# Expert layers of a four-layer graph and mixture-of-experts kernel: wide first-layer products, summed on VectorE, two tiles ahead

## The reference

```
probs = softmax(xf @ gate_w + gate_b); top2_vals, top2_idx = top_k(probs, 2)
h = gelu(xf @ w1 + bb1)                # per expert: 256 -> H
y = h @ w2 + bb2                       # H -> 256
acc = acc + we[:, None] * y            # weight of this expert, 0 where it was not chosen
```

## Time and profile before

| | |
|---|---|
| median of three runs | 2801.65 us (2794.58 to 2802.57) |
| profiled execution: its own time, its span | 2792.34 us, 2790.5 us |
| TensorE busy | 2187.1 us, 78% |
| VectorE busy | 1557.0 us, 56% |
| ScalarE busy | 1131.6 us, 41% |
| GpSimd busy | 445.6 us, 16% |
| mean granted TensorE clock | 0.89 |

### The profile page before, as it was taken

One profiled execution on the slowest core, in us unless ns is written; L12 is line 12 of the kernel. 1 busy time (PEld: TensorE's weight loads), 2 busy tenths in 40 slices (PEclk: granted clock), 3 DMA queues, 4 the chain that ended last, 5 costly groups with the idle time before them and its releaser, 6 DMA issues. The chain is left out here.

```text
span 2790.5 us, 46760 instructions
## 1 busy us (share of the span) xinstructions
PE 2187.1 (78%) x16458; PEld 1556.5 (56%) x16458; DVE 1557.0 (56%) x2971; ACT 1131.6 (41%) x2510; POOL 445.6 (16%) x464
## 2 busy tenths in 40 slices
PE   6898284999999996299846885499756979797587
PEld 3687152688888885277625664377532535353233
DVE  4665634454444666722267774522366888887533
ACT  5454373311111333455436664355442323232344
POOL 0000552000000000844310003444200000000200
PEclk9999596799999998599968998699867989898689
DMA  4897365146556553422254652322213222221000
GB/s 127 275 355 262 108 139 206 60 194 249 203 212 247 207 238 135 144 63 64 57 143 108 159 142 84 100 62 64 82 47 114 73 86 73 60 73 40 31 0 40
DMA packets 211970, 357.67 MB, mean 128 GB/s; under 512 B 18681, under 2 KB 165754, under 8 KB 197051
## 3 DMA queue, kind: packets, MB, share of 16 engines
q1 hardware_dynamic: 189118, 310.39, 33.2%
q0 software_dynamic: 13152, 35.93, 4.8%
q10 hardware_dynamic: 9504, 8.65, 1.0%
HBM read 291.81 MB, written 63.12 MB: 127 GB/s over the span
## 5 line engine op out<-in xcount | busy, mean ns | idle before, releaser
L882 PE MATMUL ps<-R,BIG 128*128 128x256 f16 (+1 forms) x1936 | 533.1, 275 | 23.1 <-DVE BIG L1358 13.4
L883 PE MATMUL ps<-R,BIG 128*128 128x256 f16 x1936 | 529.3, 273 | 0.0
L884 PE MATMUL ps<-R,BIG 128*128 128x256 f16 (+1 forms) x1936 | 529.3, 273 | 0.0
L2267 PE MATMUL ps<-BIG 128*128 128x452 f32 x1056 | 408.1, 550 | 50.0 <-DVE R L2389 31.8
L2267 PEld LDWEIGHTS ps<-BIG 128*128 128x128 f32 x1056 | 203.4, 193 | 254.4 <-issue 233.3
L1796 DVE TENSOR_TENSOR X<-X 128x512 f16<-128x512 f32 (+1 forms) x152 | 84.4, 556 | 396.0 <-ACT X L1774 396.0
L882 PEld LDWEIGHTS ps<-R,BIG 128*128 128x128 f16 x1936 | 188.1, 97 | 58.9 <-DVE BIG L1358 13.7
L1769 ACT ACTIVATE X<-ps,cols 128x128 f32<-128x128 f32 x452 | 138.4, 379 | 173.8 <-PE ps L262 172.8
L2298 ACT ACTIVATE BIG<-X,BIG 128x64 f32 (+1 forms) x264 | 88.8, 336 | 295.3 <-PE ps L2267 295.3
L260 PE MATMUL ps<-X,BIG 128*128 128x128 f16 x904 | 202.2, 229 | 4.1 <-issue 2.4
L883 PEld LDWEIGHTS ps<-R,BIG 128*128 128x128 f16 x1936 | 190.7, 98 | 23.4
(11 more groups left out here) (345 smaller groups left out, 4604.3 us busy)
## 6 DMA issues: line engine op xcount, KB each, us to landing
BIG<-adj_split SPq DMA_DIRECT2D x66, 1408.0 KB, 12.8
BIG<-in_adjT SPq DMA_DIRECT2D x42, 1408.0 KB, 12.0
adj_split<-BIG SPq DMA_DIRECT2D x22, 1408.0 KB, 13.1
BIG<-in_adj SPq DMA_DIRECT2D x22, 1408.0 KB, 5.9
BIG<-in_adjT SPq DMA_DIRECT2D x66, 452.0 KB, 3.3
BIG<-in_f SPq DMA_DIRECT2D x88, 256.0 KB, 3.0
BIG<-expert_out SPq DMA_DIRECT2D x44, 256.0 KB, 3.0
rows_split<-row ACTq DMA_DIRECT2D x66, 128.0 KB, 3.8
```

The source lines that it names most:

```text
L882: pe.matmul(out[:, 0:n], pr[:, 0, k, :], h[:, k, 0:n], start=start, stop=False)
L883: pe.matmul(out[:, 0:D], pr[:, 0, k, :], l[:, k, 0:D], start=False, stop=False)
L884: return pe.matmul(out[:, 0:n], pr[:, 1, k, :], h[:, k, 0:n], start=False, stop=stop)
L2267: mm = pe.matmul(ps[:, 2 * h + c, 0:CW], self.G[:, u, h * P:(h + 1) * P], self.PT[:, u, h, c * CW:(c + 1) * CW], start=start, stop=stop)
```

## The change

In hidden, TensorE sends both halves of xf through the high weights in one product 256 columns wide, and the high half alone through the low weights, 128 wide, onto the first 128 columns. So a block of hidden columns now takes 256 columns of PSUM, of which the left and the right 128 are still to be summed. VectorE does that with one reduction for each tile (add, L1800), from PSUM into hact, and ScalarE applies the function to hact in place (L1773). The hidden banks are now 2 to 5, two for each tile, and the result banks 6 and 7. A new semaphore, ad, counts the additions; TensorE's hidden waits for it in place of ha, ScalarE's hidden in place of hm and lo, and add waits for hm and lo.

The first layer's products of a tile now run two tiles ahead of the second layer's: hidden(j+2), then result(j). turn(j+3) stands ahead of hidden(j+2). VectorE's order is add(j+2), result(j), low(j+2). The load of the expert numbers stands inside hidden, at each even tile. New lines: turn L1712, wide product L1727, narrow L1729, turned L1763, activation L1773, rounding L1778, low L1805, result copy L1811.

```diff
                     s.wait(pe, "xf", j + 1)
-                    s.wait(pe, "ha", j - 1)
+                    s.wait(pe, "ad", j - 1)
                     for t in range(HT):
+                        out = ps[:, 2 + 2 * u + t // 2, t % 2 * 2 * P:(t % 2 + 1) * 2 * P]
                         for f in range(FT):
                             w = dyn((t0 + t) * P, P)
-                            mm = mm3(pe, ps[:, 2 + u, t * P:(t + 1) * P], W1h[:, f, w], W1l[:, f, w],
-                                     xf[:, u, f, :], xf[:, u, 2 + f, :], start=f == 0, stop=f == FT - 1)
+                            pe.matmul(out.rearrange("p (h c) -> p h c", h=2), W1h[:, f, w], xf[:, u, f::2, :],
+                                      start=f == 0, stop=False)
+                            mm = pe.matmul(out[:, 0:P], W1l[:, f, w], xf[:, u, f, :], start=False, stop=f == FT - 1)
                     mm.then_inc(s["hm"], 1)
...
-                    out = ps[:, 4 + u, 0:D]
+                    out = ps[:, 6 + u, 0:D]
...
+                for j in range(J):
+                    if j + 3 < J:
+                        turn(j + 3)
+                    if j + 2 < J:
+                        hidden(j + 2)
+                    result(j)
...
-                    s.wait(act, "hm", j + 1)
-                    s.wait(act, "lo", j - 1)
+                    if j % 2 == 0:
+                        e[j], e[j + 1], _ = self.experts(act, j)
+                    s.wait(act, "ad", j + 1)
                     for t in range(HT):
-                        sc = cols[:, dyn(e + _COLS["L0_half"], 1)] if E == E0 else 1.0
-                        op = act.activation(hact[:, u, t, :], ps[:, 2 + u, t * P:(t + 1) * P], self.func,
-                                            bias=cols[:, dyn(e * HT + (self.b1 + t), 1)], scale=sc)
+                        sc = cols[:, dyn(e[j] + _COLS["L0_half"], 1)] if E == E0 else 1.0
+                        op = act.activation(hact[:, u, t, :], hact[:, u, t, :], self.func,
+                                            bias=cols[:, dyn(e[j] * HT + (self.b1 + t), 1)], scale=sc)
...
+                for j in range(J):
+                    if j + 3 < J:
+                        turned(j + 3)
+                    if j + 2 < J:
+                        hidden(j + 2)
...
+                def add(j):
+
+                    u = j % 2
+                    s.wait(v, "hm", j + 1)
+                    s.wait(v, "lo", j - 1)
+                    z = ps[:, 2 + 2 * u:4 + 2 * u, :].rearrange("p b (t h c) -> p (b t) c h", t=2, h=2)[:, 0:HT]
+                    v.tensor_reduce(hact[:, u, 0:HT, :], z, AX.X, ALU.add).then_inc(s["ad"], 1)
...
+                for j in range(2):
+                    add(j)
+                    low(j)
+                for j in range(J):
+                    if j + 2 < J:
+                        add(j + 2)
                     result(j)
-
+                    if j + 2 < J:
+                        low(j + 2)
```

More of the change, by code:

```diff
@@ L1644, in __init__ @@
                 J = self.J
-                self.st = Stage("seq", **{f"g{u}": 16 * len(range(u, J, 4)) for u in range(4)}, t3=J, xf=J, hm=J, ha=J, hi=J, lo=J,
+                self.st = Stage("seq", **{f"g{u}": 16 * len(range(u, J, 4)) for u in range(4)}, t3=J, xf=J, hm=J, ad=J, ha=J, hi=J, lo=J,
                                 ym=J, yo=J, **{self.out(u): 16 * len(range(u, J, 4)) for u in range(4)})
@@ L1713, in turn, with hidden @@
                     mm.then_inc(s["t3"], 1)
-                def hidden(j, e):
-                    u, t0 = j % 2, first(e)
+                def hidden(j):
+                    u = j % 2
+                    if j % 2 == 0:
+                        e[j], e[j + 1], _ = self.experts(pe, j)
+                    t0 = first(e[j])
                     s.wait(pe, "xf", j + 1)
-                    s.wait(pe, "ha", j - 1)
+                    s.wait(pe, "ad", j - 1)
                     for t in range(HT):
+                        out = ps[:, 2 + 2 * u + t // 2, t % 2 * 2 * P:(t % 2 + 1) * 2 * P]
@@ L1724, in hidden, with result @@
                     mm.then_inc(s["hm"], 1)
-                def result(j, e):
-                    u, t0 = j % 2, first(e)
+                def result(j):
+                    u, t0 = j % 2, first(e[j])
                     s.wait(pe, "lo", j + 1)
                     s.wait(pe, "yo", j - 1)
-                    out = ps[:, 4 + u, 0:D]
+                    out = ps[:, 6 + u, 0:D]
                     for t in range(HT):
                         mm3(pe, out, hh[:, u, t, :], hl[:, u, t, :], W2h[:, t0 + t, :], W2l[:, t0 + t, :], start=t == 0)
-                    sel = selE[:, dyn(e * P, P)]
+                    sel = selE[:, dyn(e[j] * P, P)]
@@ L1734, in result @@
                     pe.matmul(out, sel, b2h[:, self.b2, :], start=False, stop=False)
                     pe.matmul(out, sel, b2l[:, self.b2, :], start=False, stop=True).then_inc(s["ym"], 1)
-                J = self.J
                 turn(0)
                 turn(1)
[L1740 to L1750, removed]
+                hidden(0)
@@ L1752, in act @@
+                turn(2)
+                hidden(1)
+                for j in range(J):
[4 more added lines that the diff above has]
+                    result(j)
             def act(self, act):
                 after(act, self.route)
-                s, E, HT = self.st, self.E, self.HT
+                s, E, HT, J, e = self.st, self.E, self.HT, self.J, {}
                 def turned(j):
@@ L1774, in hidden @@
                     act.activation(hh[:, u, 0:HT, :], hact[:, u, 0:HT, :], ACT.Copy).then_inc(s["hi"], 1)
-                J = self.J
                 turned(0)
                 turned(1)
[L1779 to L1788, removed]
-            def dve(self, v):
-                s, HT = self.st, self.HT
+                hidden(0)
+                turned(2)
+                hidden(1)
+                for j in range(J):
[3 more added lines that the diff above has]
+                        hidden(j + 2)
+            def dve(self, v):
+                s, HT, J = self.st, self.HT, self.J
+                def add(j):
+                    u = j % 2
+                    s.wait(v, "hm", j + 1)
+                    s.wait(v, "lo", j - 1)
+                    z = ps[:, 2 + 2 * u:4 + 2 * u, :].rearrange("p b (t h c) -> p (b t) c h", t=2, h=2)[:, 0:HT]
+                    v.tensor_reduce(hact[:, u, 0:HT, :], z, AX.X, ALU.add).then_inc(s["ad"], 1)
                 def low(j):
@@ L1801, in result @@
                         s.wait(v, self.out(j % 4), 16 * (j // 4))
[L1802 to L1807, removed]
+                    v.tensor_copy(yo[:, j % 4, :], ps[:, 6 + j % 2, 0:D]).then_inc(s["yo"], 1)
+                for j in range(2):
[4 more added lines that the diff above has]
+                        add(j + 2)
                     result(j)
+                    if j + 2 < J:
+                        low(j + 2)
         class TopRows:
```

4 lines of the change are left out of this document (3 added, 1 removed).

## The result

The changed kernel takes 2891.24 us, the median of four runs (2885.79 to 2894.82), against 2798.11 us before (2790.91 to 2802.57). The ratio is 1.0334, with a 95% interval of 1.0302 to 1.0365. It is slower. The forecast was 2781 us with a range of 2764 to 2832, so the measured time lies outside the range. The profiled execution took 2893.81 us, with a span of 2892.0 us and a mean granted clock of 0.875.

A forecast was written before the change was run, and what follows sets the result against it. TensorE bounds layers 1 and 2 at 4.25 us a tile; the change makes a 4.00 us VectorE-ScalarE ring the bound. Gains of 9.7, 9.9 and 1 us, about 21, give 2801.65 - 21 = 2781 us, range 2764 to 2832.

The forecast's parts named there:

- GpSimd needs 97.8 / 50 = 2 us a tile: GpSimd in the expert stages: its busy time per tile, 2 us, was said to fit beside the VectorE-ScalarE ring.
- A: VectorE's add in PSUM: strided read costs 1.77 ns an element, add 1.96 us, total 2864 us; chance 0.18.
- one product less is issued, at 0.06 us: TensorE's first layer: each of eight groups a tile saves 0.06 us, 0.48 us a tile.
- TensorE's tile: TensorE in layers 1 and 2: its own time per tile falls from 4.25 to about 3.77 us.
- rival C: TensorE stays near 4.25 us, or hand-overs cost 0.05 more each: period 4.2, no difference, 2801 us; chance 0.18.
- The addition: VectorE's add, 128x1024 from PSUM: 1.22 us in layers 1 and 2, 0.42 in layer 0.
- Four activations from SBUF: ScalarE's first-layer activations, reading SBUF instead of PSUM: 1.28 us for four, against 1.14 from PSUM.
- The ring of both engines: VectorE and ScalarE, layers 1 and 2: add, activations, copy and low form a 4.00 us turn that becomes the bound.
- layer 0 at 1.81 us: Layer 0: the ring of VectorE and ScalarE gives 1.81 us a tile against 1.85, a gain of 1 us.
- The clock near 1: TensorE's granted clock was expected to stay near 1 after the change.
- the cheaper first layer: TensorE's first layer: wide products save 0.48 us a tile, so the period falls by 0.25 to the ring's 4.00.

## Why the prediction was wrong

**The step that failed** is the sentence "GpSimd needs 97.8 / 50 = 2 us a tile" in the paragraph on what fits beside the ring. It weighed GpSimd by its busy time and did not follow its program order; the wait of TensorE's transposes for it stood at nothing in the sum. The change moved turn one tile earlier past result, and the instruction that turn waits for, the gather, stands on another engine behind a scatter that waits for VectorE's copy. The rows to price it were in the trace of before. The scatter of the copy at 1262.95 and the gather behind it:

```profile
1263.65 0.99 POOL L1691 DMA_INDIRECT expert_out<-X,idxs  x1 [1.57 <-DVE X L1802]
1264.95 0.97 POOL L1677 DMA_INDIRECT X<-rows_split,idxg  x1 [0.30 <-issue]
...
X<-rows_split,idxg POOLq DMA_INDIRECT x152, 3.0
```

The last row is from the list of transfers: 3.0 us from a gather's issue to its landing. With 0.70 from the copy to the scatter, 1.30 to the gather, 3.0 for the landing, 2.34 for the first layer and 1.55 for the second the ring is 8.9 us before the transposes and the last hand-over are counted, an estimate of 4.4 us a tile, already above the 4.25 of before. The steady waits in the trace of before could not show it, since the old order had a tile to spare. The prediction searched for rings between VectorE and ScalarE and stopped there; of the rivals none was this one, and A, the only one well on the slow side, had another cause. The runs put this step at 2891.24 - 2782.55 = 109 us, the slower clock that came with it included.

**A term that was mis-sized.** The "one product less is issued, at 0.06 us", for each group, 0.48 a tile, was taken from the step from L260 to L261. With that product left out the group stayed at 0.25 to 0.26. In the earlier trace rows the steps were 0.06, 0.07 and 0.13: the two register operations had fixed the group's length and the second product fell into a gap between them. With the gathers moved, TensorE's tile is 4.18, against a forecast of 3.77 and 4.26 before, and the order without wide products is at 4.19 already. With the order and the gathers in place the wide products give at most a few us: 0.9943 with them and 0.9966 without, with intervals that overlap, and stages within 1 us of each other. So rival C's mechanism, that the wide product saves no issue, was the true one for this term.

**What was right.** The addition takes 1.218 us from PSUM (forecast 1.22), and 0.411 at the least and 0.418 at the median in layer 0 (0.42):

```profile
L1800 DVE TENSOR_REDUCE X<-ps x152: 411/1218/1226, 333.9 to 2099.0; 128x512 f32<-128x1024 f32 x100, 128x128 f32<-128x256 f32 x52
```

Rival A, the strided read, is dead: 1024 elements cost 1.04 ns each over the fixed 150 ns, as in contiguous rows, so the cacheline rule of the Trainium skill ("Advanced Engine Details and Errata", Memory Cachelines) does not show in this instruction. Four activations from SBUF take 1.28 us as summed, by the timeline of the changed kernel:

```profile
1304.38 1.28 ACT L1773 ACTIVATE X<-X,cols 128x128 f32<-128x128 f32 x4 [3.62 <-DVE X L1800]
```

By the figures of the Trainium skill, "VectorE: DVE Perf Modes", section on the TRN2 errata, the estimate was 1.31; the trace does not reach it. The ring of both engines is 4.02 where nothing else holds it (forecast 4.00). The forecast said layer 0 at 1.81 us; it stayed at 1.85. The clock near 1 did not hold in the changed kernel (0.90 over layer 1), but it did, at 1.00 between 1200 and 1370, in the runs with wide products or the new order and no gather ring. It was at 0.92 in the narrow kernel with the ring, so it came with the waits, not with the wide products.

That the kernel with the gathers moved comes to 2782.55 us, beside the forecast's 2781, is chance in part: the period fell by 0.10 in place of 0.25, and the order brought it, not the cheaper first layer of the forecast. The copies of layers 1 and 2 span 199.5 and 199.1 us in it against 206.7 and 207.0. In layer 1, 5.4 of the 7.2 us are in the first 47 spacings and 1.8 in the last two, the shorter end of a layer whose first products are already done.

## What to carry to other kernels

When a step is moved ahead on one engine, follow every instruction that it waits for to its own queue and write down what stands in front of it there: a ring may close through an engine that is busy for less than half of the time, and the trace of before shows nothing of it while there is a tile to spare. Count a ring's length and divide it by the number of tiles that it spans, before and after the move. A product between two register operations may be free, so a step between two starts is no price of the instruction: take the group's whole length and ask which of its members sets it.

## What the runs showed of the hardware

A matrix product with a register operation ahead of it starts about 0.13 us after the one before it, 128 or 256 columns wide; without register operations the starts are 0.055 and 0.11 us apart, at a granted clock of 1.00. A load of the expert numbers into registers costs TensorE 0.65 us by the lengths of tiles with and without it and 0.8 by the periods, while the timeline above shows 0.22 us of it as waiting for issue. A reduction over two PSUM elements 512 bytes apart runs at the rate of contiguous reads from PSUM, 1.04 ns an element. After a wait of 2.41 us TensorE's granted clock fell, and products 256 columns wide started 0.21 us apart in place of 0.11.
